# One perceiver layer on one core: attention scores as 64-row products in two banks, the column term as a single fp32r product, the first norm placed earlier, and the correction's rows moved

## The chip, the cores and the metric

The kernel runs on one core of a Trainium2 chip. Its engines are TensorE (PE in the profile, with its weight loads as PEld), VectorE (DVE), ScalarE (ACT), GpSimd (POOL) and SyncE (SP), which issues nearly all transfers. The metric is the device time of one execution in microseconds; smaller is better.

## The reference

Three stages on x (2 batches of 128 rows by 2048), each added to x after a layernorm of it:

```python
x = x + fake_quant(LN(x)) @ fake_quant(ctx)            # ctx: 2 x 2048 x 2048, scales and zero points are inputs
q = LN(x) @ Wq                                         # 32 heads of 64
k, v = LN(x) @ Wkv                                     # one k and one v of 64 columns, shared by all heads
scores = q k^T / 8 + slope_h * (pos_k - pos_q), causal
x = x + softmax(scores) v @ Wo
W = scales[row // 128] * (nibble(qweight) - nibble(qzeros) - 1)
x = x + LN(x) @ W + bias
```

## The kernel before, in words

**Queues.** Every engine runs a list that is written out by hand. Semaphores carry the order between engines, each engine runs its own list strictly in order, and a wait holds up all that stands behind it.

**First stage (the context).** 32 tiles of ctx (1 MiB each) come in through a ring of 8 buffers. ACT rounds a tile to uint8 (`round_ctx`, L411), DVE converts it to bf16 (`convert_ctx`, L679, two buffers q16, so tile i waits until PE is through with tile i-2), and PE multiplies it (`ctx_tile`: four products L956 into four banks and four products L963 of ones with 32 output rows each, which collect the tile's column sums in one bank). The zero point of the row operand enters afterwards: `colsums(b)` copies the column sums (L685), and `zero_point(b)` adds, for each of the four banks, one full fp32 product (L970) of the copy with `sel`, a matrix that has the value 128 minus zero point in one row. After it DVE adds each bank to x (`first_residual`, L690), takes statistics (L597) and normalises (L611); PE transposes the result (`transposes(n)`, L988), ACT copies the transposes rounded to fp32r (`upper`, L424) and DVE the remainder (`remainder`, L618). Batch 0's `transposes(0)` stand inside the loop over batch 1's tiles, ahead of tile 8; on DVE `normalise(0)` stands behind `convert_ctx(KT + 4)`; ACT has its first two `upper(0, g)` behind tile 25. The Wq tiles use half of the ctx ring as their buffers.

**Attention.** Wq and Wo come as 16 granules each (4 k-tiles by 512 columns) in a ring of 4 (5 for Wo). A granule is split in ACT (`upper_w`, L433, rounded) and DVE (`remainder_w`, L627), and PE makes three fp32r products of 512 columns per k-tile (L995 to L997; for Wq's first four granules L1008 and L1015). `keys_values` (L1041 to L1047) computes k and v, transposed. DVE writes them to `kv_t`, ACT's queue copies k to both halves of `k_t` by two transfers (L521), and ACT then builds `k_pair` (L526): for each batch 256 columns, of which the first 128 have k in rows 0 to 63 and zeros below, the other 128 k in rows 64 to 127 and zeros above. For each of 8 units (4 groups of 8 heads, 2 batches) PE transposes q (L1064), computes the scores of 8 heads by four fp32 products of 128 rows by 256 columns (`scores`, L1076), DVE adds the position term (`biased_scores`, L783) and takes maxima (L791), ACT exponentiates (L462), DVE divides (`over_sum`, L798), PE transposes the probabilities (L1088) and multiplies with v (`attend`, L1100: two products, one for output rows 0 to 63, one for 64 to 127). Units ua = 2n-2 and ub = 2n-1 of group n stand between the granules:

```python
                q_granule(w + 1, 0)
                scores(ua)
                q_granule(w + 1, 1)
                scores(ub)
                q_granule(w + 2, 0)
                q_granule(w + 2, 1)
                probs_t(ua)
```

**Last stage.** Wo's granules, then 16 tiles of the 4-bit weights, which DVE multiplies out (L865, L870) while PE multiplies (L1138). The zero points' part and the bias come in as one product (`correction`, L1171) with `corr`, rows of scales times (7 - nibble) plus the bias row. `corr` lies in `work`, which the probabilities use too, so its rows are zeroed (POOL, L395 and L396) and loaded (SP, L320 and L321) after the attention (`attention_over`); DVE unpacks and multiplies them (L884, L887, L888) in one run ahead of `second_residual(1, 0)`.

## Time and profile before

| | |
|---|---|
| median of 3 runs | 424.68 us (423.73 to 426.18) |
| profiled execution | 425.28 us, of which the span (first to last instruction) 423.4 us |
| TensorE's granted clock, mean over the span | 0.992 |
| PE / weight loads / DVE / ACT busy | 374.8 / 275.9 / 318.5 / 223.6 us |

The span is what the trace's times are in, counted from the first instruction; 1.88 us of the profiled execution lie outside it. Busy shares are means over stages with different limits, so the stages are to be read one by one: up to some 96 us transfers, ACT, DVE and PE share the work; behind that PE is nearly always busy.

### The profile page before, as it was taken

How to read it: one execution, taken by the hardware profiler on the slowest of the kernel's cores; microseconds unless marked ns; L12 is line 12 of the kernel's file. 1: busy time of each engine (PE TensorE's matmuls, PEld its weight loads, DVE VectorE, ACT ScalarE, POOL GpSimd, SP SyncE). 2: the span in 40 equal slices, each digit the busy share in tenths (PEclk: the TensorE clock that was granted, in tenths of full speed). 3: DMA queues.
4: the chain of work that ended last, by engine and by line, in shares of the span. 5: the costliest groups of instructions: out<-in, count | busy, mean ns of one | idle time of the engine just before them, and what ended most of it. 6: DMA issues, size and time to landing. Idle time of an engine off the chain costs nothing.

```text
span 423.4 us, 4567 instructions
## 1 busy us (share of the span) xinstructions
PE 374.8 (89%) x1772; PEld 275.9 (65%) x1772; DVE 318.5 (75%) x354; ACT 223.6 (53%) x268; POOL 9.2 (2%) x43
## 2 busy tenths in 40 slices
PE   0167595878898999999999999999999999999996
PEld 0112131325786877877877867888888788888884
DVE  2598989768963394594595786679999899999922
ACT  1898888795334495297377465336605234444000
POOL 6000000000000000000000002000000000000000
PEclk9998999999999999999999999999999999999999
DMA  8999999995083294393436520987400000000033
GB/s 325 426 423 421 418 421 423 420 392 201 4 293 113 99 231 167 123 249 125 167 132 206 190 100 2 318 231 294 195 0 2 0 2 0 0 2 0 2 99 99
DMA packets 24273, 77.43 MB, mean 183 GB/s; under 512 B 1626, under 2 KB 1802, under 8 KB 19210
## 3 DMA queue, kind: packets, MB, share of 16 engines
q1 hardware_dynamic: 24084, 77.01, 50.4%
q8 instruction: 14, 0.23, 0.2%
q10 hardware_dynamic: 168, 0.13, 0.1%
q14 instruction: 7, 0.06, 0.0%
HBM read 74.91 MB, written 2.10 MB: 182 GB/s over the span
## 4 chain that ended last, share of the span: by engine, by line
PE 74%; DVE 16%; ACT 4%; issue 3%; DMA 2%; ACTq 0%; DVEq 0%
PE bank L1138 20%; PE bank L995 12%; PE bank L997 11%; PE bank L996 11%; DVE q L679 5%; PE bank L956 4%; PE bank L1076 3%; DVE stats L597 2%; PE bank L1008 2%; PE bank L1100 2%; ACT q L411 2%; PE bank L1015 2%; PE bank L1088 1%; DMA prm_row<-in_L_xattn_x_zp 1%; DVE resid L690 1%
## 5 line engine op out<-in xcount | busy, mean ns | idle before, releaser
L627 DVE TENSOR_TENSOR w_lo<-raw,w_hi 128x2048 fp32r<-128x2048 f32 x29 | 65.9, 2285 | 12.2 <-ACT w_hi L433 12.2
L433 ACT ACTIVATE w_hi<-raw 128x2048 fp32r<-128x2048 f32 x29 | 55.2, 1912 | 27.8 <-DMA raw<-in_L_attn_Wo 15.6
L1138 PE MATMUL bank<-w_hi,hd 128*128 128x512 f32 x208 | 52.6, 390 | 0.0
L956 PE MATMUL bank<-q,at 128*128 128x512 bf16 x128 | 36.8, 414 | 16.6 <-DVE q L679 16.3
L1138 PEld LDWEIGHTS bank<-w_hi,hd 128*128 128x128 f32 x208 | 39.0, 188 | 8.1
L679 DVE TENSOR_SCALAR q<-q 128x2048 bf16<-128x2048 uint8 x32 | 38.4, 1218 | 6.4 <-PE bank L963 3.6
L995 PE MATMUL bank<-w_hi,xt 128*128 128x512 f32 x96 | 40.1, 417 | 1.6 <-ACT work L443 1.6
L995 PE MATMUL bank<-w_hi,hd 128*128 128x512 f32 x104 | 41.3, 398 | 0.0
L997 PE MATMUL bank<-w_hi,hd 128*128 128x512 f32 x104 | 40.5, 390 | 0.0
L996 PE MATMUL bank<-w_lo,hd 128*128 128x512 f32 x104 | 40.5, 389 | 0.0
L462 ACT ACTIVATE work<-work,neg_mx 128x128 f32<-128x128 f32 x64 | 24.8, 390 | 26.3 <-DVE neg_mx L791 26.1
L997 PE MATMUL bank<-w_hi,xt 128*128 128x512 f32 x96 | 37.6, 391 | 0.0
L996 PE MATMUL bank<-w_lo,xt 128*128 128x512 f32 x96 | 37.4, 390 | 0.0
L411 ACT ACTIVATE q<-raw,prm,inv 128x2048 uint8<-128x2048 f32 x16 | 33.3, 2090 | 2.5 <-DMA raw<-in_ctx 2.4
L411 ACT ACTIVATE q<-ctx_more,prm,inv 128x2048 uint8<-128x2048 f32 x16 | 32.5, 2086 | 1.2 <-DMA ctx_more<-in_ctx 1.2
L956 PEld LDWEIGHTS bank<-q,at 128*128 128x128 bf16 x128 | 10.6, 102 | 34.6 <-DVE q L679 20.5
L783 DVE SCALAR_TENSOR_TENSOR work<-kq,bank 128x128 f32<-128x128 f32 x64 | 13.3, 282 | 22.9 <-PE bank L1076 22.9
L559 ACT ACTIVATE work<-work 128x4096 bf16<-128x4096 uint16 x5 | 18.1, 3615 | 21.9 <-DVE work L858 21.9
L1138 PE MATMUL bank<-w_lo,hd 128*128 128x512 f32 x104 | 28.8, 389 | 0.0
L995 PEld LDWEIGHTS bank<-w_hi,xt 128*128 128x128 f32 x96 | 18.0, 188 | 7.5 <-issue 2.4
L995 PEld LDWEIGHTS bank<-w_hi,hd 128*128 128x128 f32 x104 | 19.5, 188 | 4.7 <-issue 0.8
L997 PEld LDWEIGHTS bank<-w_hi,hd 128*128 128x128 f32 x104 | 19.5, 188 | 4.1
(148 smaller groups left out, 625.0 us busy)
## 6 DMA issues: line engine op xcount, KB each, us to landing
raw<-in_ctx SPq DMA_DIRECT2D x16, 1024.0 KB, 16.8
ctx_more<-in_ctx SPq DMA_DIRECT2D x16, 1024.0 KB, 17.2
raw<-in_L_attn_Wq SPq DMA_DIRECT2D x16, 1024.0 KB, 5.8
raw<-in_L_attn_Wo SPq DMA_DIRECT2D x13, 1024.0 KB, 5.2
raw_fifth<-in_L_attn_Wo SPq DMA_DIRECT2D x3, 1024.0 KB, 7.3
resid<-in_x SPq DMA_DIRECT2D x2, 1024.0 KB, 11.7
scale<-in_L_ffn_scales SPq DMA_DIRECT2D x16, 128.0 KB, 6.7
packed<-in_L_ffn_qweight SPq DMA_DIRECT2D x2, 1024.0 KB, 7.4
```

What stands on the lines that cost most here:

```text
L411: nc.scalar.activation(q8[:, i % Q8], ctx_slots[i % CTX_RING], ACT.Identity, bias=prm[:, 3:4], scale=inv[:, 2:3]).then_inc(ctx_q, 1)
L433: nc.scalar.activation(hi_slots[s], raw_slots[s], ACT.Copy).then_inc(w_hi_set, 1)
L462: ins = nc.scalar.activation(prob[:, c], prob[:, c], ACT.Exp, scale=-1.0, bias=neg_mx[:, u % 2, h:h + 1], accum_out=den[:, u % 2, h:h + 1])
L559: nc.scalar.activation(values.bitcast(BF16), values.bitcast(U16), ACT.Copy, bias=-8.0).then_inc(d8_set, 1)
L627: nc.vector.tensor_tensor(lo_slots[s], raw_slots[s], hi_slots[s].bitcast(F32), ALU.subtract).then_inc(w_lo_set, 1)
L679: nc.vector.tensor_scalar(q16[:, i % 2], q8[:, i % Q8], -QSHIFT, None, ALU.add).then_inc(ctx_c, 1)
L783: ins = nc.vector.scalar_tensor_tensor(out=prob[:, c], in0=kq[:], scalar=-sl[2 * PAIRS * g + r], in1=bank[:, SCORE_BANK + r // PAIRS, r % ...
L956: mm(bank[:, 4 * b + n, :], at[:, k, b * P:(b + 1) * P], q16[:, i % 2, n * CH:(n + 1) * CH], start=start, stop=False)
L995: mm(bank[:, out_bank, :], x_hi, hi[:, c], start=first, stop=False)
L996: mm(bank[:, out_bank, :], x_hi, lo[:, c], start=False, stop=False)
L997: return mm(bank[:, out_bank, :], x_lo, hi[:, c], start=False, stop=last)
L1138: return mm(bank[:, 4 * b + n, :], left[:, j, b * P:(b + 1) * P], right[slot_of(W_F + j)][:, n * CH:(n + 1) * CH], start=part == 0 and j = ...
```

## The change

- `scores`: eight fp32 products of 64 rows by 128 columns in place of four of 128 rows by 256. The products of the even heads read rows 0 to 63 of qt and k_t and write one bank, those of the odd heads rows 64 to 127 and the other bank. `k_pair`, its zeroing on POOL and ACT's wait and two copies go.
- The column term: `colsum` holds in the lower 16 rows of each 32-row block the rounded column sum (as upper part) and in the upper rows the remainder; `sel` has the zero point difference, split in two parts, in the rows that pick them. Both are fp32r, so each L970 product is one fp32r product. `colsums` is two DVE instructions that read the bank, and `selector` grows.
- `normalise(0)` stands two conversions earlier on DVE, `transposes(0)` ahead of tile 5 on PE. `transposes(1)` has four banks of its own and no longer waits for a remainder. `q_by_upper(0, 0)` stands ahead of `zero_point(1)`, `q_by_lower(3, 0)` ahead of `keys_values`.
- The correction's rows have a place of their own, which is free once Wq's products are done: they are zeroed and loaded between Wo's granules 4 and 5, their unpacking is spread between `remainder_w`s, and the bias rows load ahead of granule 12.

```diff
-        colsum_at = work[:, 0, 2 * CH:3 * CH]
-        corr = work[:, 0]
-        corr_z = work[:, 1]
+        corr = corr_rows[:]
+        corr_z = nib_a[:]
+        corr_up = work[:, 0].bitcast(F32R)
 ...
-            return 1 + g % 3 if n == 1 else 4 * (n % B) + g
+            return (1, 2, 3, 5)[g] if n == 1 else 4 * (n % B) + g
 ... (SP)
-            for w in range(W_O, W_O + 11):
+            for w in range(W_O, W_O + 12):
                 load_granule(wo_rows, W_O, w)
+                if w == W_O + RING:
+                    sp.wait_ge(corr_zero, 1)
+                    for blk in range(3):
+                        r = slice(CBLK * blk, CBLK * blk + GROUPS)
+                        sp.dma_start(zraw[r, :], qzeros).then_inc(corr_loaded, 16)
+                        sp.dma_start(corr[r, :], scales).then_inc(corr_loaded, 16)
             sp.wait_ge(corr_set, 1)
             (the two bias rows)
+            for w in range(W_O + 12, W_O + 14):
+                load_granule(wo_rows, W_O, w)
+            attention_over(sp)
+            sp.dma_start(packed[:, 0, :], qweight[0:P, :]).then_inc(packed_loaded[0], 16)
 ... (POOL)
+            nc.gpsimd.iota(row_no[:], pattern=[[0, 1]], base=0, channel_multiplier=1).then_inc(sel_rows, 1)
+            (memset and four affine_selects on sel_at, memset on sel_col)
-            nc.gpsimd.memset(k_pair[:], 0.0).then_inc(k_zero, 1)
-            attention_over(pool)
+            pool.wait_ge(k_dup, 2 * 16)
+            pool.wait_ge(w_used, USED.index(W_O - 1) + 1)
             link(nc.gpsimd.memset(zraw.bitcast(F32), 0.0))
             nc.gpsimd.memset(corr, 0.0).then_inc(corr_zero, 1)
 ... (ACT)
-            act.wait_ge(k_dup, 2 * 16)
-            act.wait_ge(k_zero, 1)
-            for a in range(2):
-                nc.scalar.activation(k_pair[a * DH:(a + 1) * DH, :, a, :], ...).then_inc(k_set, 1)
             q_rows(1)
-            nc.scalar.activation(corr_r[:], corr, ACT.Copy).then_inc(corr_hi, 1)
-            upper_w(W_O + 14)
+            attention_over(act)
+            nc.scalar.activation(corr_up, corr, ACT.Copy).then_inc(corr_hi, 1)
+            for w in range(W_O + 13, W_O + 16):
+                upper_w(w)
 ... (DVE, selector)
-                nc.vector.memset(sel[:], 0.0).then_inc(sel_zero, 1)
-                for n in range(NCH):
-                    ins = nc.vector.tensor_scalar(sel[r, n, :], sel[r, n, :], dif[r, 1:2], None, ALU.add)
+                (row_no & 16, lower_row, dif_hi, dif_lo, sel_col in two steps: six small instructions)
+                for n in range(NCH):
+                    ins = nc.vector.tensor_scalar(sel[:, n, :], ones16[:], sel_col[:, n:n + 1], None, ALU.mult)
 ... (DVE, colsums)
-                nc.vector.tensor_copy(colsum_at, bank[:, COLSUM_BANK[b], :]).then_inc(colsum_out, 1)
+                link(nc.vector.tensor_copy(colsum_hi[:], bank[:, COLSUM_BANK[b], :]))
+                nc.vector.scalar_tensor_tensor(out=colsum[:], in0=colsum_hi[:].bitcast(F32), scalar=lower_row[:],
+                                               in1=bank[:, COLSUM_BANK[b], :], op0=ALU.mult,
+                                               op1=ALU.add).then_inc(colsum_out, 1)
 ... (DVE, order: convert KT+2, norm 0, convert KT+3 to KT+6, remainder(0, g) with KT+7 to KT+9 between)
 ... (DVE: the correction's three steps with remainder_w(W_O + 8), (W_O + 9), (W_O + 10) behind them)
 ... (PE, scores)
-                    pe.wait_ge(k_set, 2)
+                    pe.wait_ge(k_dup, 2 * 16)
                 for t in range(PAIRS):
-                    ins = mm(bank[:, SCORE_BANK + t // 2, (t % 2) * 2 * P:(t % 2 + 1) * 2 * P],
-                             qt[:, b, t, :], k_pair[:, b].rearrange("p a k -> p (a k)"), start=True, stop=True)
+                    for a in range(2):
+                        d = slice(a * DH, (a + 1) * DH)
+                        ins = mm(bank[:, SCORE_BANK + a, t * P:(t + 1) * P], qt[d, b, t, :],
+                                 k_t[d, b * P:(b + 1) * P], start=True, stop=True)
 ... (PE, order)
-                if k == KT // 2:
+                if k == 5:
                     transposes(0)
                 ctx_tile(1, k)
+            q_by_upper(0, 0)
             zero_point(1)
-            for w in range(3):
+            for w in range(1, 3):
                 q_by_upper(w, 0)
             transposes(1)
 ...
             q_by_upper(3, 1)
+            q_by_lower(3, 0)
             keys_values()
-            q_by_lower(3, 0)
```

## Rows read from the trace of the kernel before

**Rows 1.** The page: the span.
```profile
span 423.4 us, 4567 instructions
```

**Rows 2.** A stretch: length, then busy time (instructions) of PE, PEld, DVE, ACT, POOL; clock; transfers.
```profile
261.00:343.00 82.00, 80.98 (x373) 67.03 (x372) 71.67 (x70) 36.80 (x26) 1.58 (x1) 1.00 0.40 134
```

**Rows 3.** Timeline of ACT, 64 to 93 us: start, length, instruction, [idle before <- releaser].
```profile
73.97 2.10 ACT L411 ACTIVATE q<-raw,prm,inv 128x2048 uint8<-128x2048 f32 x1 [0.40 <-DMA raw<-in_ctx]
...
78.94 1.08 ACT L424 ACTIVATE xt<-bank 128x512 fp32r<-128x512 f32 x2 [2.88 <-PE bank L988]
...
84.84 8.05 ACT L411 ACTIVATE q<-ctx_more,prm,inv 128x2048 uint8<-128x2048 f32 x4
```

**Rows 4.** The chain that ended last, 95 to 106 us: start, length, what.
```profile
95.63 0.70 DVE work L685
...
104.47 1.34 DVE work L611
```

**Rows 5.** Timeline of PE, 96 to 110 us.
```profile
96.37 3.70 PE L970 MATMUL bank<-work,sel 128*128 128x512 f32 x8 [0.80 <-DVE work L685]
99.51 6.04 PE L1008 MATMUL bank<-w_hi,xt 128*128 128x512 f32 x24
105.86 1.62 PE L988 MATMUL bank<-ident,work 128*128 128x128 f32 x12 [0.31 <-DVE work L611]
108.67 0.71 PE L988 MATMUL bank<-ident,work 128*128 128x128 f32 x4 [1.18 <-DVE xt L618]
```

**Rows 6.** PE by stretch: length, busy (instructions), granted clock, transfers' share and GB/s.
```profile
36.00:38.20 2.20, 0.00 (x0) 0.90 1.02 425
38.20:40.60 2.40, 2.37 (x9) 0.50 1.00 416
...
54.30:55.50 1.20, 1.20 (x17) 0.79 0.95 396
63.50:66.10 2.60, 0.00 (x0) 1.00 1.04 432
```

**Rows 7.** Who waited for whom, PE, 96 to 140 us: total, times, longest.
```profile
PE bank L995 <- ACT work L443: 1.6, 1, 1.6
```

**Rows 8.** The chain that ended last, 130 to 137 us.
```profile
134.95 0.42 ACT k_pair L526
```

**Rows 9.** The chain: 16 bf16 transposes; one product of 256 columns; one unit's scores.
```profile
54.28 1.27 PE bank L947 x16
...
124.61 0.12 PE bank L1044
...
142.77 1.73 PE bank L1076 x8
```

**Rows 10.** Timeline of PE around one attend.
```profile
157.63 0.39 PE L997 MATMUL bank<-w_hi,xt 128*128 128x512 f32 x1
157.95 1.08 PE L1100 MATMUL bank<-prob_t,v_rows 128*64 128x512 f32 x4
...
159.30 0.39 PE L996 MATMUL bank<-w_lo,xt 128*128 128x512 f32 x1
```

**Rows 11.** Timeline of DVE, then of PE, from group 1's scores to its first probs_t.
```profile
144.53 1.67 DVE L783 SCALAR_TENSOR_TENSOR work<-kq,bank 128x128 f32<-128x128 f32 x8 [8.57 <-PE bank L1076]
152.63 1.22 DVE L798 TENSOR_TENSOR work<-work,rden 128x1024 f32<-128x1024 f32 x1
...
154.25 1.03 PE L1088 MATMUL bank<-ident,work 128*128 128x128 f32 x8
```

**Rows 12.** Who waited for whom, PE, 225 to 345 us.
```profile
PE bank L995 <- DVE xt L627: 0.8, 1, 0.8
```

**Rows 13.** Timeline of SP: the load of Wo's granule 12.
```profile
278.27 0.39 SPq L296 DMA_DIRECT2D raw<-in_L_attn_Wo  x1
```

**Rows 14.** Timeline of DVE: the remainder of granule 10 and of the last weight tile.
```profile
279.98 2.29 DVE L627 TENSOR_TENSOR w_lo<-raw,w_hi 128x2048 fp32r<-128x2048 f32 x1 [2.67 <-ACT w_hi L433]
...
399.52 2.29 DVE L870 TENSOR_TENSOR w_lo<-work,scale 128x2048 fp32r<-128x2048 bf16 x1
```

More of the change, by code:

```diff
@@ L87, in perceiver @@
             pass
+        with nc.sbuf_tensor("corr_pad", [P, 3, D], F32), nc.sbuf_tensor("corr_rows", [P, D], F32) as corr_rows:
+            pass
         xt = sb("xt", [P, 2, KT, B * P], F32R)
@@ L111, in perceiver @@
         prob_t = sb("prob_t", [P, 2, 2 * CH], F32)
-        k_pair = sb("k_pair", [P, B, 2, P], F32)
-        sb("packed_end", [P, CH], F32)
-        with nc.sbuf_tensor("sel", [P, NCH, P], F32) as sel:
+        sb("packed_end", [P, 2 * CH], F32)
+        with nc.sbuf_tensor("sel", [P, NCH, P], F32R) as sel, nc.sbuf_tensor("colsum_hi", [P, CH], F32R) as colsum_hi, \
+                nc.sbuf_tensor("colsum", [P, CH], F32R) as colsum:
             pass
@@ L202, in perceiver @@
         ctx_mm = sem("ctx_mm")
-        sel_zero = sem("sel_zero")
+        sel_rows = sem("sel_rows")
         sel_set = sem("sel_set")
@@ L357, in _ @@
                                     pattern=[[-1, P]], channel_multiplier=1).then_inc(idents_set, 1)
+            nc.gpsimd.iota(row_no[:], pattern=[[0, 1]], base=0, channel_multiplier=1).then_inc(sel_rows, 1)
+            link(nc.gpsimd.memset(sel_at[:], 0.0))
+            for part in range(2):
+                for half in range(2):
+                    link(nc.gpsimd.affine_select(out=sel_at[:, part], in_=sel_at[:, part], compare_op=ALU.not_equal,
+                                                 fill=1.0, base=-(part + 16 * half), pattern=[[-P // NCH, NCH]],
+                                                 channel_multiplier=1))
+            nc.gpsimd.memset(sel_col[:], 0.0).then_inc(sel_rows, 1)
             link(nc.gpsimd.iota(kv_t[:, P:2 * P].bitcast(I32), pattern=[[1, P]], base=0, channel_multiplier=-1))
@@ L522, in _ @@
             upper_w(6)
-            act.wait_ge(k_dup, 2 * 16)
-            act.wait_ge(k_zero, 1)
-            for a in range(2):
-                nc.scalar.activation(k_pair[a * DH:(a + 1) * DH, :, a, :],
-                                     k_t[a * DH:(a + 1) * DH, :].rearrange("p (b k) -> p b k", b=B),
-                                     ACT.Copy).then_inc(k_set, 1)
             q_rows(1)
@@ L560, in less_eight @@
                                      bias=-8.0).then_inc(d8_set, 1)
-            for w in range(W_O + 6, W_O + 14):
+            for w in range(W_O + 6, W_O + 13):
                 upper_w(w)
             act.wait_ge(bias_loaded, 16 * 2)
-            nc.scalar.activation(corr_r[:], corr, ACT.Copy).then_inc(corr_hi, 1)
-            upper_w(W_O + 14)
-            upper_w(W_O + 15)
+            attention_over(act)
+            nc.scalar.activation(corr_up, corr, ACT.Copy).then_inc(corr_hi, 1)
+            for w in range(W_O + 13, W_O + 16):
+                upper_w(w)
             less_eight(0)
@@ L726, in _ @@
             convert_ctx(KT + 2)
-            convert_ctx(KT + 3)
-            convert_ctx(KT + 4)
             reciprocal_sd(2)
             normalise(0).then_inc(norm_set, 1)
-            for i in range(5, 8):
+            for i in range(3, 7):
                 convert_ctx(KT + i)
@@ L735, in _ @@
                 if g < 3:
-                    convert_ctx(KT + 8 + g)
-            for i in range(11, 14):
+                    convert_ctx(KT + 7 + g)
+            for i in range(10, 14):
                 convert_ctx(KT + i)
@@ L783, in biased_scores @@
                     ins = nc.vector.scalar_tensor_tensor(out=prob[:, c], in0=kq[:], scalar=-sl[2 * PAIRS * g + r],
-                                                         in1=bank[:, SCORE_BANK + r // PAIRS,
-                                                                  r % PAIRS * P:(r % PAIRS + 1) * P],
+                                                         in1=bank[:, SCORE_BANK + r % 2,
+                                                                  r // 2 * P:(r // 2 + 1) * P],
                                                          op0=ALU.mult, op1=ALU.add)
@@ L875, in _ @@
             second_residual(0, 1)
-            for i in range(7, 11):
-                remainder_w(W_O + i)
+            remainder_w(W_O + 7)
             dve.wait_ge(corr_loaded, 16 * 6)
@@ L897, in _ @@
             dve.wait_ge(corr_hi, 1)
-            nc.vector.scalar_tensor_tensor(out=corr_r[:], in0=corr_r[:].bitcast(F32), scalar=part_lo[:, 0:1],
+            nc.vector.scalar_tensor_tensor(out=corr_r[:], in0=corr_up.bitcast(F32), scalar=part_lo[:, 0:1],
                                            in1=corr, op0=ALU.mult, op1=ALU.add).then_inc(corr_split, 1)
@@ L969, in zero_point @@
                 for n in range(NCH):
-                    mm(bank[:, 4 * b + n, :], sel[:, n, :], colsum_at, start=False,
+                    mm(bank[:, 4 * b + n, :], sel[:, n, :], colsum[:], start=False,
                        stop=True).then_inc(ctx_done, 1)
@@ L983, in transposes @@
                         rows = work[:, b, :].rearrange("m (h p j) -> m h j p", h=HALVES, j=PACK)[:, h, j, :]
-                    if n < B and t == 12:
-                        pe.wait_ge(lo_out, 4 * n + 1)
+                    if n == 0 and t == 12:
+                        pe.wait_ge(lo_out, 1)
                     if n == 1 and t == 0:
```

32 lines of the change are left out of this document (17 added, 15 removed).

## The prediction

> **What bounds the kernel now.** I read the page first, then the chain that ended last, then busy time by stage, and last the timelines at the places that the diff touches. Most of the span of 423.4 us [rows 1] is PE's in the chain; what matters is which stretch has it. Up to 96 us it passes between ACT, DVE and PE, and beneath them lies the stream of ctx tiles: ACT takes 2.09 us for one, but tile 25 found ACT waiting 0.40 us for its transfer [rows 3], and at 416 to 425 GB/s [rows 6] a tile of 1.05 MB takes some 2.5 us. From there on PE sets the end: in 261 to 343 us it is busy 80.98 of 82.00 us [rows 2]. So an edit pays if it ends the context stage earlier, takes a wait out of PE's list, or shortens PE's own work; nothing that only eases DVE, ACT or POOL pays behind 96 us.
>
> **End of the context stage.** Tile 25 was there at 73.97, and six tiles of 2.49 us later, at 88.9, tile 31 is. ACT took it up at 90.9: its last four tiles run back to back and end at 92.89, because ACT had stood 2.88 us for the transposes [rows 3]. With `transposes(0)` three tiles earlier this wait goes, and ACT can be at tile 31 when it lands, so at most 2.0 us are to be had. Against that DVE gets more: `colsums(0)` reads the bank twice (0.70 us [rows 4] becomes about 1.45) and `selector` gains six small instructions, some 0.6 us in all, my estimate. Both are covered by the 0.4 us per tile that ACT has over the transfers; without that cover they would cost 1.4 us. DVE's last conversions have hardly any slack once ACT no longer waits. I take 1.5 us saved, bounds 0 and 2.0. `zero_point(0)` gets shorter too, but DVE's residuals set the pace there: nothing. POOL's new small instructions lie in the first microseconds, long before the selector: nothing.
>
> **From the last tile to transposes(1).** Before, the column sum's copy took 0.70 us [rows 4], the eight fp32 passes of `zero_point(1)` 3.70 us, and DVE's chain over four residuals and the norm released `transposes(1)` at 105.86; its last four waited another 1.18 us for a remainder [rows 5]. As fp32r each of the four products should take what L1008's do, 0.23 us, so 2.8 us of PE work go. But PE was nearly level with DVE there (0.31 us of waiting at 105.86 [rows 5]), and DVE's chain doesn't get shorter. Its start: before, 0.70 for the copy and 1.14 for the first fp32 product; now `q_by_upper(0, 0)` stands ahead, 8 x 0.227 = 1.82 us, which covers the copy of 1.45, and then one product with its latency, about 0.4. So the chain starts some 0.35 us later. The removed wait gives back 1.5 us: 16 transposes at 0.109 are 1.74 us, while 105.86 to the end of the last at about 109.1 was 3.24. Sum: 1.15 us saved. Bounds 0.5 and 1.5.
>
> **The hole that this opens.** The 2.8 us of work taken from PE turn into waiting. After the last tile PE has 1.82 + 0.9 + 3.64 = 6.4 us of work and DVE's chain takes 10.6, so PE stands idle for some 4 us before `transposes(1)`. In 36.0 to 38.2 us PE did nothing, and in the next 2.4 us the granted clock was 0.50, which is 1.2 GHz; in 63.5 to 66.1 it did nothing either and the clock stayed at 1.00 [rows 6]. A hole of 4 us is longer than both, so I expect the lower level behind it, over a stretch like that of 2.4 us or a little more, in which half the work is lost: 1.3 us against the change. Bounds 0 and 1.7. DVE and ACT don't make it good, since `q_by_upper(0, 1)` then needs PE's transposes split.
>
> **Keys, values and the second drain.** PE stood 1.6 us for ACT's copy of the second q bank [rows 7], because that copy stood behind the wait for the k transfers and two `k_pair` copies; the first of these started at 134.95, when the transfer had landed [rows 8]. Now ACT goes from the transfers' issue to `upper_w(6)` and on to the copy. `keys_values` moves behind `q_by_lower(3, 0)` and so ends 0.9 us later, and all that depends on it (v's transposes, the k transfers, `upper_w(6)`) with it; I get 0.1 us of waiting before `value_rows` and 0.15 before the second granule. Saved: 1.3 us, bounds 1.0 and 1.6. `scores(0)` at 142.77 is far behind the k transfer.
>
> **The scores.** One unit is 1.73 us [rows 9]: four products as two passes each, 8 x 0.216 for 256 columns. Now there are 16 passes of 128 columns, 0.108 each. One after another they come to the same 1.73; the question is whether those on rows 0 to 63 run beside those on rows 64 to 127. The trace has no such pair. The nearest row is `attend`, two products with 64 output columns each: one after another their four passes of 512 columns would be 4 x 0.43 = 1.73 us, but from the L997 slot's end (157.63 + 0.23) to the L996 behind, less one slot (159.30 - 0.23), there are only 1.21 us [rows 10]. So halves by columns do run side by side, in 0.86 us, with 0.35 us for going in and out. For halves by rows I take the same 0.35. A pass and its weight load, both of 128 fp32 columns, can't go faster than L1044's step, whose product streams for as long as its load: 0.12 us [rows 9]. Eight steps are 0.96, the unit 1.31, so 0.42 less. Bounds: 1.06 (steps of 0.108, 0.2 around them), 0.67 less; and 16 x 0.12 + 0.35 = 2.27 if loads or products take turns, 0.54 more. I stay with the side-by-side value, since the row it is nearest to has it.
>
> The Trainium skill (TensorEngine Tiling (Array Packing), Key Properties) says that different tiles can load and multiply in parallel, but that changing the tiling mode drains TensorE. The attend row agrees with both, its 0.35 us being the drain. By the first alone a unit would take 0.96, with the second it comes out as above.
>
> Not all of it arrives. DVE's chain from `scores(ua)` ends at 152.63 + 1.22 = 153.85 and PE wants the result at 154.25 [rows 11]: 0.40 us of slack. What `scores(ua)` saves moves both; what `scores(ub)` saves moves PE alone, up to 0.40. So three groups give 0.42 + 0.40 = 0.82 each. In group 4 PE already waits 0.8 us for a remainder that DVE makes behind the same chain [rows 12], so only `scores(ua)` counts there, 0.42. Sum 2.9 us, bounds 3.9 saved and 4.3 lost.
>
> **The correction.** Its 5.75 us of DVE go into gaps in which DVE waits for Wo's granules, such as the 2.67 us ahead of 279.98 [rows 14]. That frees DVE, not PE: nothing. The price is on SP: granules 12 to 15 and the packed weights now stand behind the wait for the unpacked rows, which I put at about 279.7, with the bias rows ahead, so granule 12 loads at 280.4 and not 278.27 [rows 13]. PE reaches granule 12 near 295 us. Nothing, and 2 us if that cover were gone. POOL's zeroing and the six row loads stand ahead of granule 5's load, whose buffer comes free some 5 us later.
>
> **Sum.** 1.5 + 1.15 - 1.3 + 1.3 + 2.9 = 5.55 us. The profiled execution of 425.28 us (span 423.4 and 1.88 around it) would become 419.7; it lies 0.6 above the median, so the median becomes 424.68 - 5.5 = 419.2 us. DVE ends its weight tiles at 401.8 [rows 14] and shifts with PE, since its run of work from 280 us starts when PE frees buffers.
>
> **Rivals.** Shares without the scores come to 2.65 us.
> - *Row halves side by side* (forecast): 419.2, from 415.8 with all upper bounds to 421. Chance 0.60; the attend row speaks for it.
> - *Held back by small passes.* 16 bf16 transposes took 1.27 us, 0.079 each, though at a granted clock of 0.79 [rows 6, 9]. If 16 passes kept that pace, a unit is 1.27 + 0.35 = 1.62, 0.11 less: 4 x 0.11 + 3 x 0.11 = 0.8 us, and the time is 421.2. Chance 0.18. The Trainium skill (TensorE: Matmul & The Clock Gate, Back-to-back issue gap) states 81 ns for each product of 128 columns with its load; the trace's 0.079 agrees, at a mixed clock.
> - *They take turns.* 2.27 us a unit: 4.3 us lost, 1.7 us over before, 426.3. This is also "it doesn't do what it says". For it: nothing in the trace shows two row halves at once. Chance 0.14.
> - *Slower: loads laid open.* If in this form a half's load doesn't hide behind its other pass, each of the 16 passes costs load and product, 0.24: 3.84 + 0.35 = 4.2 a unit, 2.5 x 8 = 20 us lost, 442 us. It decides from 2.06 us a unit on, where the other savings are eaten. Against it: L1044's load hides wholly. Chance 0.05.
> - *A wait that replaces those removed* (DVE late in the context stage, granule 12 late): costs up to 2 to 3 us, time 421 to 422.5. Chance 0.03.
>
> Half a per cent, 2.1 us, is what a measurement here can tell from no change. Faster: the first two and the last, less their tails, 0.79. Same: most of the take-turns case, 0.14. Slower: 0.07. The range takes in the small-pass case and the better edge of the take-turns case above, and the full savings below: 415.5 to 424.0.
>
> **What the changed profile would show.** Right: L1076's successor as passes near 0.27 us that start in pairs, a unit in 1.2 to 1.4 us; ACT's last tile ending near 91; L970 as four products in 0.9 us; a hole of about 4 us before `transposes(1)` with a clock of 0.50 behind it; no wait of L995 for L443 over 0.3 us; and a new wait of PE at `probs_t(ua)` under 0.1 us. Wrong if: a unit takes 1.7 us or more; ACT's last tile ends at 92 or later; PE waits for granule 12 or for `q_by_upper(0, 1)`'s remainders; or DVE's chain in a group sets PE's pace.

## The result, and the profile after

The changed kernel takes 421.39 us (median of 7 executions, 419.38 to 421.66), the kernel before in the same comparison 425.55 us (7 executions, 423.73 to 426.87). The ratio is 0.9892 with a 95% interval of 0.986 to 0.9923: some 1.1% faster. The forecast was 5.5 us less, and 4.2 came; the sign and the range held. The profiled execution took 421.66 us, of which the span is 419.9. So the spans differ by 3.5 us, and this is the sum that has to be taken apart.

The page of the changed kernel, its span and the rows of busy time:

```profile
span 419.9 us, 4691 instructions
...
PE 369.7 (88%) x1823; PEld 272.1 (65%) x1828; DVE 320.4 (76%) x361; ACT 223.0 (53%) x266; POOL 9.7 (2%) x49
```

PE's busy time fell by 5.1 us, the span by 3.5: part of what was taken from PE's work came back as standing. I go through the stretches in order of time. First the end of the context stage, ACT's timeline from 76 to 92 us:

```profile
76.06 1.06 ACT L438 ACTIVATE xt<-bank 128x512 fp32r<-128x512 f32 x2
...
86.45 2.09 ACT L425 ACTIVATE q<-ctx_more,prm,inv 128x2048 uint8<-128x2048 f32 x1 [0.36 <-DMA ctx_more<-in_ctx]
88.98 2.10 ACT L425 ACTIVATE q<-ctx_more,prm,inv 128x2048 uint8<-128x2048 f32 x1 [0.43 <-DMA ctx_more<-in_ctx]
```

and PE's from 65 to 113 us:

```profile
65.34 0.62 PE L979 MATMUL bank<-q,ones 128*32 128x512 bf16 x4 [4.82 <-DVE resid L706]
...
73.40 1.62 PE L1004 MATMUL bank<-ident,work 128*128 128x128 f32 x12
77.41 1.12 PE L1004 MATMUL bank<-ident,work 128*128 128x128 f32 x4 [2.39 <-DVE xt L627]
...
95.54 2.11 PE L1024 MATMUL bank<-w_hi,xt 128*128 128x512 f32 x8
97.48 1.07 PE L986 MATMUL bank<-colsum,sel 128*128 128x512 f32 x4
...
106.24 3.68 PE L1004 MATMUL bank<-ident,work 128*128 128x128 f32 x16 [4.06 <-DVE work L620]
109.57 3.06 PE L1024 MATMUL bank<-w_hi,xt 128*128 128x512 f32 x8
112.48 1.08 PE L1031 MATMUL bank<-w_lo,xt 128*128 128x512 f32 x4
```

ACT does what was forecast: it is at the last tile when this lands, and is through at 91.08 in place of 92.89. PE isn't: it leaves the stage at 95.6, as before. The rows tell why. `transposes(0)`'s last four want DVE's first remainder, for this DVE wants ACT's first `upper` copy, and ACT makes that between two tiles. PE stands 2.39 us there, in the middle of the stage, and DVE after it, since its next conversion wants the buffer that PE hasn't read:

```profile
76.66 0.69 DVE L627 TENSOR_TENSOR xt<-bank,xt 128x512 fp32r<-128x512 f32 x1 [1.84 <-ACT xt L438]
80.91 1.23 DVE L692 TENSOR_SCALAR q<-q 128x2048 bf16<-128x2048 uint8 x1 [3.55 <-PE bank L979]
...
91.66 2.53 DVE L692 TENSOR_SCALAR q<-q 128x2048 bf16<-128x2048 uint8 x2 [0.25 <-PE bank L979]
```

From there on DVE goes from conversion to conversion with hardly a gap, behind ACT all the time. The bound of this end is DVE and PE handing two buffers to each other, and no longer ACT.

PE by stretch (length, busy time, granted clock, transfers) shows what the holes do to the clock:

```profile
65.30:70.60 5.30, 5.26 (x20) 0.50 1.01 422
77.40:80.20 2.80, 2.57 (x11) 0.52 1.01 418
102.20:106.20 4.00, 0.00 (x0) 0.83 0.00 0
106.20:109.90 3.70, 3.66 (x17) 0.50 0.02 4
109.90:112.60 2.70, 2.70 (x10) 0.67 0.00 0
```

The hole ahead of `transposes(1)` is 4.06 us. Behind it PE has the lower level, 1.2 GHz, for all 16 transposes, and a mixture for the eight products behind them. In the chain the two take 3.68 and 2.72 us; experiment 4 below, which keeps the clock, has 2.08 and 1.84 there. That is 2.5 us lost in this execution; experiment 9, whose code is the same up to here, loses less behind a hole of the same length. It leaves the rest of this stretch as forecast: `transposes(1)` starts 0.38 us later than before, and the removed wait gives 1.45 (105.86 to 109.14 in the kernel before is 3.28 us, and 1.83 in experiment 4); 0.38 - 1.45 + 2.5 is the 1.4 us that the kernel lost there.

The chain at the scores, and PE's timeline around the first of them:

```profile
142.81 1.09 PE bank L1095 x16
```

```profile
142.43 0.39 PE L1013 MATMUL bank<-w_hi,xt 128*128 128x512 f32 x1
142.74 1.16 PE L1095 MATMUL bank<-k_t,qt 64*128 64x128 f32 x16
143.84 0.50 PE L1011 MATMUL bank<-w_hi,xt 128*128 128x512 f32 x1
144.17 0.39 PE L1012 MATMUL bank<-w_lo,xt 128*128 128x512 f32 x1
...
161.03 1.03 PE L1107 MATMUL bank<-ident,work 128*128 128x128 f32 x8
...
190.59 1.03 PE L1107 MATMUL bank<-ident,work 128*128 128x128 f32 x8
...
220.16 1.03 PE L1107 MATMUL bank<-ident,work 128*128 128x128 f32 x8
...
251.05 1.03 PE L1107 MATMUL bank<-ident,work 128*128 128x128 f32 x8
```

One L1013 starts at 142.43 and has a slot of 0.23; L1012 starts at 144.17 with one slot of L1011 ahead of it. So the unit and its edges take 144.17 - 0.23 - 142.43 - 0.23 = 1.28 us, where 1.31 was forecast and it was 1.73 [rows 9]. Inside the unit the passes start in pairs, as forecast, each pass 0.27 us long (the first two 0.37): the timeline, taken at single moments, has two starts each within 0.02 us of 142.74, 142.96, 143.07, 143.18, 143.29, 143.40, 143.51 and 143.63. So a step of two passes takes 0.11 us, eight take 0.90, and 0.38 us are left for the edges. At 143.28 to 143.30 six passes, three pairs, are under way:

```profile
143.07 0.50 PE L1095 MATMUL bank<-k_t,qt 64*128 64x128 f32 x6
```

From one group's second `probs_t` to the next are 29.56, 29.57 and 30.89 us; in the kernel before these lie at 161.82, 192.25, 222.68 and 254.19, which gives 30.43, 30.43 and 31.51.

Last the place where the correction used to be, DVE and then PE:

```profile
310.55 1.35 DVE L620 TENSOR_SCALAR work<-resid,mv,rstd 128x2048 f32<-128x2048 f32 x1
```

```profile
313.03 1.95 PE L1004 MATMUL bank<-ident,work 128*128 128x128 f32 x16
```

DVE is 1.1 us ahead of PE here. In the kernel before they were level: its norm (L611) ended at 316.27 and `transposes(2)` began at 316.32, which is no wait in the table of waits and no slack either (PE's last product ahead of it started at 315.93, so PE could have begun at 316.16).

The stretches, start of each taken at the same work in both traces:

| stretch | before | after | gained | forecast |
|---|---|---|---|---|
| to the end of the context stage | 95.57 | 95.54 | 0 | 1.5 |
| from there to q_by_lower(0, 0), at 111.22 and 112.64 | 15.6 | 17.1 | -1.4 | -0.15 |
| from there to the second granule behind keys_values, at 136.57 and 136.61 | 25.35 | 23.97 | 1.4 | 1.3 |
| scores, group 1 to 4 | | | 3.2 | 2.9 |
| rest of the span | | | 0.35 | 0 |
| sum | 423.4 | 419.9 | 3.5 | 5.55 |

### The profile page after: what moved, and what is told of

Same layout as the page of the kernel before. It is cut to its first block, busy times and chain, and to the rows that moved or that the text cites. A ratio compares the mean times of both kernels' runs of the same rounds, so it can differ in the third digit from the quotient of the medians.

```text
span 419.9 us, 4691 instructions
## 1 busy us (share of the span) xinstructions
PE 369.7 (88%) x1823; PEld 272.1 (65%) x1828; DVE 320.4 (76%) x361; ACT 223.0 (53%) x266; POOL 9.7 (2%) x49
## 4 chain that ended last, share of the span: by engine, by line
PE 72%; DMA 14%; DVE 9%; ACT 3%; issue 2%; ACTq 0%; DVEq 0%
PE bank L1157 20%; DMA raw<-in_ctx 12%; PE bank L1011 12%; PE bank L1013 12%; PE bank L1012 11%; PE bank L1024 3%; PE bank L1119 2%; PE bank L1095 2%; PE bank L1004 2%; ACT q L425 2%; DVE q L692 2%; PE bank L1031 2%; PE bank L1107 1%; PE bank L972 1%; DMA prm_row<-in_L_xattn_x_zp 1%
## 5 line engine op out<-in xcount | busy, mean ns | idle before, releaser
L1011 PE MATMUL bank<-w_hi,hd 128*128 128x512 f32 x104 | 41.2, 396 | 0.0
L1013 PE MATMUL bank<-w_hi,hd 128*128 128x512 f32 x104 | 40.5, 390 | 0.0
L1012 PE MATMUL bank<-w_lo,hd 128*128 128x512 f32 x104 | 40.5, 389 | 0.0
L1011 PE MATMUL bank<-w_hi,xt 128*128 128x512 f32 x96 | 39.6, 412 | 0.0
L1013 PE MATMUL bank<-w_hi,xt 128*128 128x512 f32 x96 | 37.6, 392 | 0.0
L1012 PE MATMUL bank<-w_lo,xt 128*128 128x512 f32 x96 | 37.5, 390 | 0.0
L1011 PEld LDWEIGHTS bank<-w_hi,hd 128*128 128x128 f32 x104 | 19.5, 188 | 4.8 <-issue 0.8
L1011 PEld LDWEIGHTS bank<-w_hi,xt 128*128 128x128 f32 x96 | 18.0, 188 | 6.5 <-issue 2.6
L1013 PEld LDWEIGHTS bank<-w_hi,hd 128*128 128x128 f32 x104 | 19.5, 188 | 4.2
## 6 DMA issues: line engine op xcount, KB each, us to landing
raw<-in_ctx SPq DMA_DIRECT2D x16, 1024.0 KB, 17.1
```

Source lines behind the costliest of these rows:

```text
L1011: mm(bank[:, out_bank, :], x_hi, hi[:, c], start=first, stop=False)
L1012: mm(bank[:, out_bank, :], x_hi, lo[:, c], start=False, stop=False)
L1013: return mm(bank[:, out_bank, :], x_lo, hi[:, c], start=False, stop=last)
```

## The experiments

All were timed against the kernel before, and the ratios are to it. They are worked out over all executions, so they differ a little from the ratios of the medians given here. Four of them shared one set of runs of the kernel before (424.94 us, 23 executions), four another (424.57 us, 17), the last had its own (423.34 us, 17).

**1. The scores alone.** The kernel before with the change's `scores` and nothing else; `k_pair`, its zeroing and its copies go, since nothing reads them.

```diff
-            act.wait_ge(k_dup, 2 * 16)
-            act.wait_ge(k_zero, 1)
-            (the two copies to k_pair)
 ...
-                    ins = mm(bank[:, SCORE_BANK + t // 2, (t % 2) * 2 * P:(t % 2 + 1) * 2 * P],
-                             qt[:, b, t, :], k_pair[:, b].rearrange("p a k -> p (a k)"), start=True, stop=True)
+                    for a in range(2):
+                        d = slice(a * DH, (a + 1) * DH)
+                        ins = mm(bank[:, SCORE_BANK + a, t * P:(t + 1) * P], qt[d, b, t, :],
+                                 k_t[d, b * P:(b + 1) * P], start=True, stop=True)
```

> The kernel before with the scores alone in 64-row products (and so without k_pair, its wait and its two copies on ACT). Theory: a unit's slot falls from 1.73 to about 1.3 us, three groups give 0.83 us each, the last 0.4 to 0.6, and the 1.6 us wait of PE for ACT's copy of the q bank goes with k_pair, without moving keys_values: 4.5 to 4.9 us faster than before, as much as the whole change or more. Rival: the scores need the rest of the change to pay (the q bank's wait is only shortened by the move of keys_values), 3 us or less.

Measured: 421.35 us (12 executions, 420.12 to 423.12), ratio 0.9924 (0.9896 to 0.9953), profiled span 418.6. This one part brings 0.8% of the whole change's 1.1%, and the intervals overlap. The forecast was 4.5 to 4.9 us; the medians differ by 3.6, and the profiled spans by 4.8, of which 1.2 us lie in the context stage, which the edit doesn't touch (the column sum's product starts at 95.21 and not 96.37). The unit is again 1.09 us in the chain. But PE, which came to Wo's first product 6.05 us earlier than before (241.32 against 247.37), could not bring that to the end. PE's timeline at `transposes(2)`, behind DVE's row of the norm:

```profile
310.15 1.35 DVE L603 TENSOR_SCALAR work<-resid,mv,rstd 128x2048 f32<-128x2048 f32 x1
```

```profile
311.55 2.07 PE L980 MATMUL bank<-ident,work 128*128 128x128 f32 x16 [1.29 <-DVE work L603]
```

DVE came only 4.8 us earlier. Without the 1.2 us of the context stage PE gained 4.9 us by Wo's first product and kept 3.6 at `transposes(2)`. This was the first hint that the place where DVE and PE were level matters, and that the correction's 5.75 us of DVE work ahead of it are not free.

**2. The halves in turn.** The changed kernel, with the eight products of one row half first and then those of the other:

```diff
-                for t in range(PAIRS):
-                    for a in range(2):
+                for a in range(2):
+                    for t in range(PAIRS):
                         d = slice(a * DH, (a + 1) * DH)
```

> The changed kernel with the same 64-row products in another order: first the four of rows 0 to 63, then the four of rows 64 to 127. Theory (the saving comes from two row halves running side by side, and PE takes products in order): neighbours share their rows, so a unit goes back to 16 steps of 0.11 to 0.12 and the 0.35 around them, 2.1 to 2.3 us, 0.9 longer than the 1.28 of the changed kernel; 8 units, less what DVE's slack hides, make 6 to 8 us more, so 2 to 4 us slower than before. Rival (a 64-row pass is cheaper by itself, or PE pairs them whatever the order): the unit stays at 1.3 us and the time at that of the changed kernel, 1.0% under before.

Measured: 424.3 us (12 executions), ratio 0.9993 (0.9961 to 1.0025), profiled span 423.6. The timeline at the first unit, and its passes at 143.80:

```profile
142.14 0.39 PE L1013 MATMUL bank<-w_hi,xt 128*128 128x512 f32 x1
142.46 1.71 PE L1095 MATMUL bank<-k_t,qt 64*128 64x128 f32 x16
144.10 0.50 PE L1011 MATMUL bank<-w_hi,xt 128*128 128x512 f32 x1
144.44 0.39 PE L1012 MATMUL bank<-w_lo,xt 128*128 128x512 f32 x1
```

```profile
143.56 0.50 PE L1095 MATMUL bank<-k_t,qt 64*128 64x128 f32 x3
```

The same 16 passes take 144.44 - 142.14 - 2 x 0.227 = 1.84 us in place of 1.28, and nearly all that the change gave is gone. Three passes are under way at 143.80, where the changed kernel has six. So two row halves do run side by side, nearly always when their products alternate in PE's list and seldom when they don't. The Trainium skill (TensorEngine Tiling (Array Packing), Key Properties) says that different tiles can load and multiply in parallel; these two kernels agree, and add that for most passes it takes neighbours in the list. In-turn was also cheaper than I had put it (1.84, not 2.1 to 2.3). The timeline, taken at single moments, has 13 starts for the 16 passes (142.46, 142.67, 142.79, then every 0.11 us to 143.90), since three passes in the middle, around the change of the half, start together with another. 13 steps of 0.112 and the same 0.38 for the edges are the 1.84.

One rival isn't tested by itself: the edit changes the order of the two banks along with that of the row halves. Against banks as the cause, `zero_point` in the kernel before writes another bank with each product, on all rows, and its passes of 512 columns start 0.43 us apart, so 0.108 us for 128 columns, no faster than the passes of the in-turn unit; and `attend`'s two column halves, which did run side by side [rows 10], write one bank. Whether row halves need two banks as well is open.

**3. The last four of transposes(0) later.** In the changed kernel they go behind two more tiles:

```diff
                 if k == 5:
-                    transposes(0)
+                    transposes(0, range(12))
+                if k == 7:
+                    transposes(0, range(12, KT))
```

> The changed kernel with the last four of transposes(0), which wait for DVE's remainder, moved from tile 5 to tile 7. Theory: PE's 2.4 us wait at 77.4 us and the half clock behind it are what kept the context stage from ending earlier; without them DVE's last conversion starts when ACT's last tile is done at 91, PE ends the stage near 93.8 and not 95.6, and the time falls by 1.3 to 1.8 us, to 1.35% under before. Rival: DVE's own work or the transfers set the end of the stage, it ends at 95.4 or later and the time stays.

Measured: 419.12 us (6 executions, 418.97 to 420.27), ratio 0.9867 (0.9827 to 0.9907), profiled span 418.1. The stage ends at 93.8:

```profile
93.80 2.14 PE L1024 MATMUL bank<-w_hi,xt 128*128 128x512 f32 x8
...
104.53 3.22 PE L1004 MATMUL bank<-ident,work 128*128 128x128 f32 x16 [3.26 <-DVE work L620]
```

So the gain that I had forecast at this place (1.5 us) exists, 1.7 us of it, and the wait in `transposes(0)` is what kept it away: the four profiled executions that have the wait (the changed kernel, experiments 2, 4 and 9; 1.96 to 3.11 us) end the stage at 95.06 to 95.54, while in this kernel PE has no wait there. By the trace this is shown; by the ratios alone, whose intervals overlap with the changed kernel's, it is not.

**4. The hole filled.** The changed kernel with 16 products ahead of `transposes(1)` that go to a bank which nobody reads before it is written again:

```diff
             for w in range(1, 3):
                 q_by_upper(w, 0)
+            for i in range(16):
+                mm(bank[:, 1, :], xt_hi[:, 0, 0:P], hi_slots[slot_of(2)][:, 0:CH], start=True, stop=True)
             transposes(1)
```

> The changed kernel with 16 products added ahead of transposes(1), 0.23 us each, whose result nobody reads, so that PE works through the 4.06 us in which it stood. Theory: the granted clock stays at 1.00 over the transposes (1.75 us instead of 3.68) and the eight products behind them (1.81 instead of 2.72); 2.5 to 2.9 us faster than the changed kernel, 1.6 to 1.8% under before. Rival (the transposes are slow for another reason, such as their own form or their banks): no gain, or 0.3 us lost to the added work.

Measured: 419.3 us (6 executions, 419.16 to 420.05), ratio 0.9868 (0.9829 to 0.9908), profiled span 417.4. PE's timeline:

```profile
101.88 3.79 PE L1217 MATMUL bank<-w_hi,xt 128*128 128x512 f32 x16
106.11 2.08 PE L1004 MATMUL bank<-ident,work 128*128 128x128 f32 x16 [0.44 <-DVE work L620]
107.94 2.08 PE L1024 MATMUL bank<-w_hi,xt 128*128 128x512 f32 x8
109.86 1.07 PE L1031 MATMUL bank<-w_lo,xt 128*128 128x512 f32 x4
```

`transposes(1)` starts when it did, but `q_by_lower(0, 0)` is there at 109.86 and not 112.48. Work that nobody uses makes the profiled execution 2.5 us of span shorter, and the rival (slow transposes for another reason) is excluded. But 2.5 us is the price of the hole in one execution. The forecast for the time, 1.6 to 1.8% under before, was missed (1.3%): by the ratios the filling brings 1.0 us, with intervals that overlap. In the executions of experiments 2 and 9, which have the same hole, the time from the start of `transposes(1)` to `q_by_lower(0, 0)` is 6.07 and 4.99 us, after 6.24 in the changed kernel's and 3.75 here. So the hole cost 2.5, 2.3 and 1.2 us.

**5. Both.** Experiments 3 and 4 together, with 14 products in the hole.

> The changed kernel with both mends: the last four of transposes(0) at tile 7, and 14 products that nobody reads ahead of transposes(1). Theory (the late end of the context stage and the half clock behind the hole are separate losses): the stage ends near 93.9 us and the transposes run at a granted clock of 1.00, so the two gains add up, 1.7 + 2.8 us under the changed kernel, about 2% under before (416.5 to 417.5). Rival (they share one cause, or another engine sets the pace once both are gone): no faster than the better of the two alone, 1.3% under before.

Measured: 417.57 us (6 executions, 417.51 to 417.83), ratio 0.9834 (0.9808 to 0.9859), profiled span 415.9, mean clock 0.987. It beats both kernels; its interval lies below that of the change alone. The two gains add up to 4.0 us of span, of 1.8 and 2.5 by themselves. The forecast of 416.5 to 417.5 us and about 2% was just missed (1.66%); by the ratios it is 2.5 us under the changed kernel, of 1.1 and 1.0 by themselves, which is no less than their sum.

**6. The correction back, in the kernel of experiment 5.** Rows, loads, their order on SP and DVE's run of three steps are where they were before the change:

```diff
-        corr = corr_rows[:]
-        corr_z = nib_a[:]
+        corr = work[:, 0]
+        corr_z = work[:, 1]
 ... (SP: Wo's granules 0 to 10 first)
+            attention_over(sp)
+            sp.wait_ge(corr_zero, 1)
+            (the six row loads, granules 11 to 13, packed, then the bias rows)
 ... (DVE: remainder_w(W_O + 8) to (W_O + 10) ahead of all three steps)
-            remainder_w(W_O + 8)
             link(nc.vector.tensor_scalar(corr_z[rows, :], zi, -1.0, 7.0, ALU.mult, ALU.add))
-            remainder_w(W_O + 9)
             nc.vector.tensor_tensor(corr[rows, :], corr[rows, :], corr_z[rows, :], ALU.mult).then_inc(corr_set, 1)
-            remainder_w(W_O + 10)
```

> The kernel with both mends, and the correction's rows back in their old place: loaded after the attention, unpacked on DVE in one run, the bias rows behind the packed weights. Theory A (the prediction's: it frees DVE alone): no difference from the kernel with both mends. Theory B: with PE this much earlier DVE's chain ahead of transposes(2), which had no slack before (its norm ended at 316.27 us, PE took it at 316.32), sets PE's pace, so PE waits 1 to 3 us at transposes(2) and that much is lost against the kernel with both mends.

Measured: 419.78 us (6 executions, 419.04 to 421.58), ratio 0.9888 (0.9859 to 0.9917), profiled span 418.0. PE's timeline:

```profile
310.63 2.07 PE L1000 MATMUL bank<-ident,work 128*128 128x128 f32 x16 [1.53 <-DVE work L618]
```

2.1 us of span are lost, 1.53 of them in this one wait. In experiment 5 the same transposes stand at 308.98 with no wait.

**7. The column term alone.** The kernel before with the fp32r column sum, `sel` and `selector` of the change.

```diff
-                nc.vector.tensor_copy(colsum_at, bank[:, COLSUM_BANK[b], :]).then_inc(colsum_out, 1)
+                link(nc.vector.tensor_copy(colsum_hi[:], bank[:, COLSUM_BANK[b], :]))
+                nc.vector.scalar_tensor_tensor(out=colsum[:], in0=colsum_hi[:].bitcast(F32), scalar=lower_row[:],
+                                               in1=bank[:, COLSUM_BANK[b], :], op0=ALU.mult,
+                                               op1=ALU.add).then_inc(colsum_out, 1)
```

> The kernel before with the column term alone as one fp32r product (colsum in two parts, the longer selector), all else in its old order. Theory: DVE's chain starts as late as before (1.45 + 0.4 against 0.70 + 1.14 us), so PE's 2.8 us come back as waiting ahead of transposes(1), some 2.4 us in one piece; if the granted clock falls behind it, the kernel is 1 to 2.9 us slower than before, if it does not, within 0.5 us. Rival (PE's work sets the end there too): up to 2.8 us faster.

Measured: 425.31 us (12 executions), ratio 1.002 (1.0 to 1.0039), profiled span 422.9. PE's part of `zero_point(1)` falls from 3.70 [rows 5] to 1.21 us, and nothing is gained. The clock fell behind the hole, and the ratio says 0.9 us slower, just under the 1 to 2.9 put for that case:

```profile
97.85 1.21 PE L991 MATMUL bank<-colsum,sel 128*128 128x512 f32 x4 [1.58 <-DVE colsum L704]
...
106.73 2.50 PE L1009 MATMUL bank<-ident,work 128*128 128x128 f32 x12 [2.19 <-DVE work L625]
```

**8. Experiment 3 with the column term back in fp32.** `colsums` is one copy again and `zero_point` eight fp32 passes; the rest is the change's.

```diff
-                link(nc.vector.tensor_copy(colsum_hi[:], bank[:, COLSUM_BANK[b], :]))
-                nc.vector.scalar_tensor_tensor(out=colsum[:], in0=colsum_hi[:].bitcast(F32), ...)
+                nc.vector.tensor_copy(colsum[:], bank[:, COLSUM_BANK[b], :]).then_inc(colsum_out, 1)
```

> The changed kernel with the split transposes(0) and the column term back as before (one fp32 product, one copy, the short selector); q_by_upper(0, 0) still stands ahead of zero_point(1). Theory: PE's hole ahead of transposes(1) shrinks from 3.3 us (in the kernel with the split alone) to about 1.1, the clock stays at 1.00, and DVE's chain starts 0.7 us later: 1.7 to 2.2 us faster than the kernel with the split alone, 416.9 to 417.6. Rival (the fp32r product is a gain in itself): slower than the kernel with the split alone.

Measured: 418.51 us (6 executions, 418.21 to 420.13), ratio 0.9864 (0.9835 to 0.9893), profiled span 416.4, against 419.12 and 418.1 of experiment 3.

```profile
95.72 3.59 PE L977 MATMUL bank<-colsum,sel 128*128 128x512 f32 x8
...
105.11 2.08 PE L995 MATMUL bank<-ident,work 128*128 128x128 f32 x16 [2.16 <-DVE work L620]
```

`transposes(1)` starts 0.58 us later than in experiment 3, but at the full clock, and `q_by_lower(0, 0)` stands at 108.86 and not 109.89. The other 0.7 us of the 1.7 between the spans lie behind it and have no cause here; experiment 3's profiled execution was the second longest of its six. The forecast (a hole of 1.1 us, 416.9 to 417.6 us) was missed. The medians differ by 0.6 us and the intervals overlap, so on the time alone this is inconclusive; in these two traces the fp32r column term doesn't pay unless its hole is filled.

**9. The correction back, in the changed kernel itself.** The edit of experiment 6.

> The changed kernel with the correction's rows in their old place, load order and DVE order; nothing else is touched. A, the prediction's step (the move frees DVE, not PE, and is worth nothing): span 419.9 us as after's, transposes(2) at 313.0 us without a wait, ratio to before 0.989. B, the theory from the two kernels with the early drain (there DVE's norm ended 2.5 us later with the rows in the old place, 310.58 against 308.08, and PE waited 1.53): here DVE's norm, which ends at 311.91 in the changed kernel, ends near 314.4, PE that would be there at 313.0 waits some 1.3 to 1.5 us, the span is 421.2 to 421.4 and the ratio 0.992.

Measured: 422.31 us (12 executions, 419.07 to 424.0), ratio 0.9962 (0.9933 to 0.9991), profiled span 420.6. Without the move the ratio is 0.7% worse, and the intervals don't touch. But the kernel before was itself faster in this comparison (423.34 us, after 425.55 in that of the changed kernel); the medians of the two kernels themselves, 422.31 and 421.39, differ by 0.9 us. DVE, then PE:

```profile
311.73 1.35 DVE L618 TENSOR_SCALAR work<-resid,mv,rstd 128x2048 f32<-128x2048 f32 x1
```

```profile
311.10 0.39 PE L1009 MATMUL bank<-w_hi,hd 128*128 128x512 f32 x1
313.13 2.07 PE L1000 MATMUL bank<-ident,work 128*128 128x128 f32 x16 [1.65 <-DVE work L618]
```

PE would have been there at 311.5 and waits 1.65 us. Ahead of `q_by_lower(0, 0)` this execution was 1.7 us faster than that of the changed kernel (110.76 against 112.48): it left the context stage 0.5 us earlier, and behind the same hole of 4.06 us the lower level cost it 1.2 us less.

```profile
105.77 3.33 PE L1000 MATMUL bank<-ident,work 128*128 128x128 f32 x16 [4.06 <-DVE work L618]
108.85 2.07 PE L1020 MATMUL bank<-w_hi,xt 128*128 128x512 f32 x8
```

```profile
105.70:109.00 3.30, 3.23 (x17) 0.56 0.02 5
```

So the spans, 420.6 and 419.9, hide most of the wait. Theory B holds for the wait, a little above its 1.3 to 1.5; its span (421.2 to 421.4) and ratio (0.992) came out between and beyond the two theories, at 420.6 and 0.9962. DVE's norm was put at 314.4 and ends at 313.08, because DVE too came earlier in this execution. From `transposes(2)` to the end it is 107.5 us, 0.6 more than in the changed kernel; 1.65 and 0.6 don't make up all of the 0.7% (3.0 us), and are more than the 0.9 us of the medians. So the wait is shown, and the size of the loss in time is not settled.

## Why the prediction was right, and where it was not

- **Scores: right.** The forecast row was `attend`'s two column halves, with 0.35 us for the edges, and it carried over to rows: 1.28 against 1.31 us a unit. Groups 1 to 3 gave 0.84 to 0.87 each (forecast 0.82), group 4 0.62 (forecast 0.42), with PE's wait for a remainder there grown from 0.83 to 1.05 us. The passes start in pairs, and experiment 2 shows that this is the mechanism. The terms hold too: steps of 0.112 (forecast 0.12, put as the least that a step can take) and 0.38 at the edges (forecast 0.35), in both orders.
- **The take-turns and the laid-open rivals: excluded** by the unit's time. The first happened on purpose in experiment 2, and ended at no gain. Its price had been put too high: 2.27 us a unit and 426.3 in the prediction, against 1.84 and 424.3. The rival of passes held back at 0.079 us each is excluded too: a pair takes 0.112, so 0.056 each.
- **Keys and values: right**, 1.4 against 1.3 us. The wait for the second q bank is gone, and the table of waits lists no other before group 4.
- **End of the context stage: the step that failed.** "With `transposes(0)` three tiles earlier this wait goes, and ACT can be at tile 31 when it lands" is true of ACT and worth nothing, because the same move put a longer wait on PE (2.39 us, where the kernel before had 0.51 at 80.32). I followed the engine whose wait was removed, and not the chain ACT copy, DVE remainder, PE transposes in its new surroundings, with the tiles queued behind it. The rival of a wait that replaces those removed named the context stage, at 0.03. Experiment 3 moves four instructions and gets 1.7 us in its trace.
- **The hole: mechanism right, size too small in two profiled executions of three.** Its length (4.06 us), the level behind it (0.50) and the start of `transposes(1)` (0.38 us later, forecast 0.35) came as forecast, and the removed wait gave 1.45 (forecast 1.5). The term that failed in the profiled execution is "over a stretch like that of 2.4 us or a little more": the lower level held for all of the 3.7 us that followed, and in part for 2.7 more. There it was 2.5 us in place of 1.3, outside my upper bound of 1.7, since I had bounded the loss by one earlier stretch of 2.4 us; experiment 2's execution has 2.3. But experiment 9's, with the same hole, has 1.2, and the ratios of experiment 4 give 1.0 us for the filling. So the price is not one number: it varies by more than a microsecond from one execution to the next. That the hole is the cause is shown by experiment 4, which takes it away.
- **The two together** make the fp32r column term a doubtful part of this change: 3.6 us of PE's work became 1.07, and what was saved turned into standing, since DVE's chain over the residuals was level with PE there. Experiment 7 shows that by itself it gains nothing; experiment 8 points the same way by its trace, not by its time.
- **The correction: the reason was wrong, though the sum didn't show it.** "That frees DVE, not PE: nothing" looked at 280 us, where DVE has gaps, and not at 316, where DVE and PE were level. In the kernel before it would have been worth at most the 0.16 us that PE stood ahead of 316.32, by that trace; this wasn't run. But the sum let 2.9 us of scores and 1.3 of keys go straight to the end, and they only get there because DVE's norm came 4.37 us earlier too. With the rows in their old place PE waits 1.65 us (experiment 9), 1.53 (experiment 6) and 1.29 (experiment 1). So the forecast's total for scores and keys was right by the help of a part that it had priced at zero, and that is luck.
- **The last 0.35 us** of the span are spread over two stretches behind the attention (0.15 ahead of `transposes(2)`, 0.21 behind). The first is the 0.16 us that PE stood there in the kernel before and no longer stands (312.79 + 0.23 against 313.03); for the second I can't give a cause.
- **The total.** The forecast had 5.5 us and the medians 4.2. What is missing is about the size of the context stage's 1.5 us, and the other errors (the hole, the scores, the rest) have different signs and partly cancel; a range of 8.5 us could not tell these cases apart.

Not tried: a version in which the hole of 4.8 us at 60 to 65 us is filled as well (it was 2.68 us in the kernel before, and grew because `zero_point(0)` got shorter too). PE runs at 0.50 for 5.3 us behind it. With `transposes(0)` split it doesn't show at the end of the stage: experiment 3 has the hole of 4.82 us and ends it at 93.80, experiment 8 one of 2.68 us and ends it at 93.77. Whether it does in the changed kernel is open.

## What to carry to other kernels

When a move takes a wait off one engine, walk the moved work's own chain through its new place, on every engine that it touches, before you book the gain; and look for places where two engines are level although no wait is shown there, because a saving upstream stops at them. Work taken from PE just ahead of a point where it must wait is worth less than nothing if the hole lowers the clock; give the price of the hole a wide range, from several executions, and not from one earlier stretch. Compare spans of profiled executions only beside the times of all executions: one kernel's differed by 2 us here. Products that use half the rows pay only if the two halves alternate in the list.

## What the runs showed of the hardware

- Order inside PE's list decides how much row halves overlap: 16 passes of 64 rows by 128 columns took 1.28 us alternating (8 pairs, 0.112 us a step) and 1.84 us one half after the other (13 starts), edges included. The edges to the full-row products on both sides came to 0.38 us in both.
- The clock's answer to a hole isn't a function of its length alone. Behind 4.06 us idle it was 0.50 for 3.7 us and 0.67 for 2.7 more; behind 3.26 us (experiment 3) 0.61 for 3.2 us and 0.80 for 2.3; behind 2.19 us (experiment 7) 0.61 for 2.5 us; behind 2.16 us (experiment 8) it stayed at 1.00. And with code that is the same up to there, another hole of 4.06 us (experiment 9) was followed by 0.56 for 3.3 us.

PE by stretch in experiment 7, and behind the hole in experiment 8:

```profile
104.50:106.70 2.20, 0.04 (x1) 1.00 0.00 0
106.70:109.20 2.50, 2.47 (x12) 0.61 0.00 0
```

```profile
105.10:107.20 2.10, 2.09 (x17) 1.00 0.00 0
```

- Executions of one kernel differ by this. The changed kernel's seven spans run from 417.6 to 419.9 us, the four longest at a mean clock of 0.973 or 0.974, the three shortest at 0.978 to 0.983; experiment 5, whose late hole is filled, had six times within 0.32 us. The Trainium skill (TensorE: Matmul & The Clock Gate, Part 1) says that the number of products that run at the lower level at a kernel's start differs from run to run of the same kernel; here the same is seen behind a hole in the middle, where experiments 2 and 9 and the changed kernel differ by up to 1.25 us.
